# Attention and FFN block: weighted sums in pairs in the halves of one PSUM bank, reciprocals turned in the query fills

## The reference, cut to what matters

```python
q, k, v = layernorm(x) @ wq + bq, ctx @ wk + bk, ctx @ wv + bv   # split into 16 heads
score = (q @ k.T) / sqrt(32) * mask
score = where(score == 0, -1e9, score)
x = x + (softmax(score) @ v) @ wo + bo
w = complex(w_real, w_imag)
x = x + real(ifft(fft(layernorm(x)) @ w)) + bias
```

## Time and profile before

| | |
|---|---|
| median of three runs | 472.79 us |
| the profiled execution | 471.82 us |
| its span in the profile | 470.0 us |
| mean granted TensorE clock | 0.996 of full speed |
| TensorE busy | 449.7 us, 96% |
| VectorE busy | 415.9 us, 88% |
| ScalarE busy | 373.9 us, 80% |
| GpSimd busy | 364.5 us, 78% |

### The profile page before, as it was taken

One profiled execution on the slowest core, in us unless ns is written; L12 is line 12 of the kernel. 1 busy time (PEld: TensorE's weight loads), 2 busy tenths in 40 slices (PEclk: granted clock), 3 DMA queues, 4 the chain that ended last, 5 costly groups with the idle time before them and its releaser, 6 DMA issues.

```text
span 470.0 us, 11312 instructions
## 1 busy us (share of the span) xinstructions
PE 449.7 (96%) x3538; PEld 297.8 (63%) x3538; DVE 415.9 (88%) x698; ACT 373.9 (80%) x1431; POOL 364.5 (78%) x519
## 2 busy tenths in 40 slices
PE   6989879898999999999999999999999999999997
PEld 5777557677566666666666666666666666555543
DVE  3797799999999898989999999989898999999552
ACT  3359559789998889899898988898988898899720
POOL 6589657897989979787979797987979882868562
PEclk9999989999999999999999999999999999999999
DMA  8999902332444554444544545353632432341143
GB/s 284 395 352 294 270 11 67 86 86 68 94 105 117 115 135 114 128 120 119 140 108 113 131 102 158 85 137 103 128 78 71 90 82 74 84 91 44 48 112 113
DMA packets 83308, 59.37 MB, mean 126 GB/s; under 512 B 39729, under 2 KB 70705, under 8 KB 82738
## 3 DMA queue, kind: packets, MB, share of 16 engines
q1 hardware_dynamic: 82816, 58.55, 46.2%
q10 hardware_dynamic: 434, 0.10, 0.1%
HBM read 29.27 MB, written 8.39 MB: 80 GB/s over the span
## 4 chain that ended last, share of the span: by engine, by line
PE 80%; DVE 8%; issue 4%; ACT 3%; DMA 2%; POOL 1%; SPq 0%; DVEq 0%; POOLq 0%
PE bank L396 33%; PE bank L468 16%; PE bank L522 10%; PE bank L539 7%; PE bank L401 5%; PE bank L510 5%; PE bank L535 3%; ACT zs L624 2%; DMA cxs<-in_ctx 2%; DVE zs L784 1%; DVE zs L791 1%; PE bank L471 1%; DVE nmin L796 1%; DVE lp L839 1%; POOL x L1002 1%
## 5 line engine op out<-in xcount | busy, mean ns | idle before, releaser
L624 ACT ACTIVATE zs<-zs,nbias 128x128 f32<-128x128 f32 x512 | 199.8, 397 | 19.7 <-POOL nbias L1016 19.6
L624 ACT ACTIVATION_READ_ACCUMULATOR zs<-zs,nbias 128x1 f32 x512 | 99.6, 194 | 0.0
L791 DVE SCALAR_TENSOR_TENSOR zs<-zs 128x1024 f32<-128x1024 f32 x64 | 91.8, 1435 | 2.3
L784 DVE TENSOR_TENSOR zs<-bank,ms 128x512 f32<-128x512 f32 x128 | 82.0, 682 | 0.0
L796 DVE TENSOR_REDUCE nmin<-zs 128x8 f32<-128x1024 f32 x64 | 77.2, 1206 | 0.1
L633 ACT COPY pt<-bank 128x512 f32<-128x512 f32 x128 | 67.8, 582 | 7.0 <-PE bank L522 6.8
L468 PE MATMUL bank<-xth,wqh 128*128 128x256 f16 x256 | 70.7, 276 | 2.2 <-DVE kl L743 1.8
L468 PE MATMUL bank<-xth,wql 128*128 128x256 f16 x256 | 70.2, 274 | 0.0
L468 PE MATMUL bank<-xtl,wqh 128*128 128x256 f16 x256 | 70.1, 274 | 0.0
L522 PE MATMUL bank<-ident,zs 128*128 128x128 f32 x512 | 66.9, 274 | 1.0 <-ACT zs L624 1.0
L522 PEld LDWEIGHTS bank<-ident,zs 128*128 128x128 f32 x512 | 57.4, 140 | 5.7 <-ACT zs L624 4.4
(11 more groups left out here) (109 smaller groups left out, 954.7 us busy)
## 6 DMA issues: line engine op xcount, KB each, us to landing
xs<-in_x SPq DMA_DIRECT2D x16, 512.0 KB, 4.4
xtr<-in_xt SPq DMA_DIRECT2D x16, 512.0 KB, 5.1
out<-x SPq DMA_DIRECT2D x32, 256.0 KB, 2.5
qs<-qh SPq DMA_DIRECT2D x120, 64.0 KB, 2.0
lp<-in_lparts SPq DMA_DIRECT2D x4, 1024.0 KB, 9.8
qs<-ql SPq DMA_DIRECT2D x60, 64.0 KB, 2.0
ms<-in_mask SPq DMA_DIRECT2D x16, 128.0 KB, 2.4
wqs<-in_wq SPq DMA_DIRECT2D x2, 512.0 KB, 6.4
```

The lines of the kernel that those rows point to most:

```text
L624: last = act.activation(z, z, ACT.Exp, bias=nbias[:, s % 4, i:i + 1], scale=-NEG, accum_out=zsum[:, s % 4, i:i + 1])
L784: dve.tensor_tensor(zs[:, s % NZ, t], A[n % 2][:].rearrange("p (h k) -> p h k", h=4), ms[:, c % NM, t, :].unsqueeze(1).broadcast_to([128, ...
L791: dve.scalar_tensor_tensor(out=z, in0=z, scalar=0.0, in1=z, op0=ALU.is_equal, op1=ALU.subtract).then_inc(eq_done, 1)
```

## The change

- The weighted sums are made two at a time, at the head of even slots: slot v does steps v-4 and v-3, the even step in the lower half of bank CX, the odd one in the upper half. In PE's order they now stand ahead of `turn`. `ctx_norm` of either step waits for both sums, and the next pair waits until both are normed.
- The reciprocals of step v-3 are turned at the end of the last late fill of slot v, into the upper half of that fill's bank. From slot 55 on, where no query is left, a fill `R` holds them alone.
- The upper half of query quarter 2 is no longer free, so the statistics get a fill `ST` of their own just ahead of that quarter.
- ScalarE copies the reciprocals after `copy_pt`, followed by the held fills, and only then does the second half of `exps`. VectorE does `least`, then the held fills, then `ctx_norm`, then `low_m` and the mid fills.

The core of the diff:

```diff
-        late = [("Q",) + f for f in queries.get(v, [divmod(v + 9, 4)]) if f[0] < NC]
+        late = []
+        for f in queries.get(v, [divmod(v + 9, 4)]):
+            if f[1] == 2 and 3 <= f[0] + 1 < NC:
+                late.append(("ST", f[0] + 1))
+            if f[0] < NC:
+                late.append(("Q",) + f)
+        if 0 <= v - 3 < NS and not late:
+            late.append(("R", v - 3))
...
+        if 0 <= v - 3 < NS:
+            turned[v - 3] = len(fills) - 1
         items = []
+        if v % 2 == 0 and 0 <= v - 4 < NS:
+            items += [("PV", v - 4), ("PV", v - 3)]
         if 0 <= v - 2 < NS:
             items += [("PT", v - 2, 0), ("PT", v - 2, 1)]
...
-        if 0 <= v - 3 < NS:
-            items += [("PV", v - 3)]
...
+            def turn_rz(o, s):
+                pe.wait_ge(p_rz, s + 1)
+                for t in range(2):
+                    last = pe.transpose(o[:, 256 + 128 * t:384 + 128 * t], rzb[:, s % 2, 4 * t:4 * t + 4, :], ident[:])
...
+                if n in step_of:
+                    last = turn_rz(o, step_of[n])
...
-                if s >= 1:
-                    pe.wait_ge(cn_done, s)
+                if s >= 2:
+                    pe.wait_ge(cn_done, s - s % 2)
...
-                pe.wait_ge(p_rz, s + 1)
-                for t in range(2):
-                    pe.transpose(CX[:, 256 + 128 * t:384 + 128 * t],
-                                 rzb[:, s % 2, 4 * t:4 * t + 4, :], ident[:])
+                o = slice(256 * (s % 2), 256 * (s % 2) + 256)
...
             def copy_rec(s):
-                act.wait_ge(pv_done, s + 1)
-                act.copy(rec[:, s % 2, :], CX[:, 256:512]).then_inc(rc_done, 1)
+                act.wait_ge(g_done, turned[s] + 1)
+                if s >= 2:
+                    act.wait_ge(cn_done, s - 1)
+                act.copy(rec[:, s % 2, :], G[turned[s] % 3][:, 256:512]).then_inc(rc_done, 1)
...
-                if 0 <= v - 4 < NS:
-                    copy_rec(v - 4)
                 if 2 <= v - 1 < NS:
                     exps(v - 1, 0)
                 if 0 <= v - 2 < NS:
                     copy_pt(v - 2, 0)
                     copy_pt(v - 2, 1)
+                if 0 <= v - 4 < NS:
+                    copy_rec(v - 4)
+                for n in held:
+                    hi(n)
...
-                for n in held + mids:
+                for n in mids:
                     hi(n)
...
                     zero_to_neg(v)
+                if 0 <= v < NS:
+                    least(v)
+                for n in held:
+                    lo(n)
                 if 0 <= v - 4 < NS:
                     ctx_norm(v - 4)
-                if 0 <= v < NS:
-                    least(v)
                 if 0 <= v - 9 < 4:
                     low_m(v - 9)
-                for n in held + mids:
+                for n in mids:
                     lo(n)
...
             def ctx_norm(s):
                 dve.wait_ge(rc_done, s + 1)
+                dve.wait_ge(pv_done, s - s % 2 + 2)
...
             def spread(s):
                 pool.wait_ge(rz_done, s + 1)
                 if s >= 2:
-                    pool.wait_ge(pv_done, s - 1)
+                    pool.wait_ge(g_done, turned[s - 2] + 1)
```

20 lines of the change are left out of this document (10 added, 10 removed).

## The result

The changed kernel takes 489.21 us, the median of three runs (489.07 to 490.04), against 472.79: ratio 1.0345, 95% interval 1.0314 to 1.0377. I had forecast 473.9 and a range that ended at 477.5. The change is 16.4 us slower.

A forecast was written before the change was run, and what follows sets the result against it. TensorE was taken to set the pace in slots 14 to 54, VectorE in slots 4 to 13, VectorE and ScalarE in the last. -3.6 + 5.5 - 0.6 = +1.3 us, rounded to 473.9 us; range 469.0 to 477.5.

The forecast's parts named there:

- the early slots: Slots 4 to 13: new VectorE waits for ScalarE's `od` and `high_m` cost 6.3 us, less 0.8 relief: +5.5.
- the steady slots: Slots 14 to 54, TensorE-paced: pairs save 2.7 us and a vanished product wait 0.9, together -3.6.
- the tail: From slot 55: VectorE's earlier start and two sums in a row at the end save 0.6 us (+0.3 to -1.2).
- The pair: Steady slots on TensorE: two sums in a row save 0.17 us per pair, net 0.14 (bounds -0.02 and 0.17).
- Rival 4: The pair saves nothing because the third batch drains like the first: 476.6 us, chance 0.10.
- DVE's 23.83 of work in what becomes 24.8 us still fits: Steady slots, per four slots: VectorE's work fits the shortened time, so TensorE waits there were taken as 0.
- the far bound of -4.4: Steady slots: the largest saving allowed for pairs and the vanished product wait together, against -3.6 expected.
- rival 3: Statistics slots: the query fill waits for its bank, 0.3 us in each of ten slots: 476.9 us, chance 0.17.
- The pair asks for the product of step v-5 some 1.1 us after it is there: Head of even steady slots: the product is ready before the pair, removing a wait of 0.9 us in all.

The follow-up runs named there:

- d1: d3, with ScalarE also doing `high_m` and the `od` copies ahead of `ctx_hi` in slots 4 to 12: 472.78 us.
- d3: Changed kernel; VectorE's product ahead of `least` and held fills, reciprocals ahead of `copy_pt` from slot 9, `ST` last in its slot (chunk 4: slot 5): 474.5 us.
- b2: Kernel before the change with only the new orders of ScalarE and VectorE, single sums kept: 486.21 us.
- a1: Changed kernel; in slots 4 to 12 ScalarE does `high_m` and the `od` copies ahead of `ctx_hi`: 487.33 us.
- a2: Changed kernel; `ST` placed behind the query quarter in its slot instead of ahead of it: 488.49 us.
- b1: Kernel before the change; only the statistics get their own fill, ahead of query quarter 2: 479.67 us.
- b4: b1, but `ST` stands last in its slot, and that of chunk 4 in slot 5 instead of 6: 473.31 us.
- e2: d1, but from slot 56 on the pair of sums stands behind `turn`: 472.86 us.

## Why the prediction was wrong, point by point

All three terms of the sum failed: the early slots cost 13.5 instead of 5.5, the steady slots lost 1.8 where 3.6 were to be gained, and the tail lost 2.1 where 0.6 was to be gained.

1. **The pair** was right in kind and small in size: 0.25 saved instead of 0.17, 0.19 net instead of 0.14. From the second batch to the third, that is from one sum to the next, it is 0.22, so nothing drains between the two sums. By the rule of the Trainium skill ("TensorEngine Tiling (Array Packing)", Key Properties) a change of the tile alone drains nothing; the trace agrees, with 1.00 for both sums. Rival 4 is out.
2. **The steady gain of 3.6** exists: d1 and d3 gain 4.8 there. The changed kernel doesn't have it, and the step that failed here is one sentence: "DVE's 23.83 of work in what becomes 24.8 us still fits". It took the busy time of before for an order that is not that of before. Two things were missing: 0.45 us per four slots for `least` directly behind the instruction it depends on, and `zero_to_neg` longer by 0.19 in the mean, 0.75 per four slots. What DVE fills of four slots is their length less its waits. Before, that was 25.2 - 1.2 = 24.0, as it waited 12.6 us for `qh` between 135 and 394 us. 24.0 + 0.45 + 0.75 = 25.2 is over the 24.8 that was to be had; the trace after has 25.47 from one group of four slots to the next (265.32 to 290.79), with 0.24 of waits. The single sums of b2, with 25.48, bear it out. How much each of the two things costs by itself no run shows. (A slip beside it: the far bound of -4.4 for the steady slots comes to -4.2 by its own terms, 19.5 x 0.17 and 0.9.) The 0.11 was to be seen in the earlier trace rows: the product there starts and gives way to an instruction that doesn't read it in 0.33, shorter than its own 0.42. I read such distances as the cost of an instruction, where they are also a property of the one behind.
3. **The early waits** (+5.5) were right in place and near in size: 0.74 in slots 4 to 6 and 1.00 to 1.61 in slots 9 to 12 of the trace, with 2.47 in slot 7 and 1.44 in slot 8 beyond it; 5.2 us by a1 and about 6.2 by b2. What failed is the sum around them. The ring of banks in slots 4 to 13 was priced as rival 3, at 0.3 in ten steady slots; in fact the steady slots pay 0.8 for its place (a2), and one early slot pays 3.1 to 3.8 at once (`U` of slot 7 behind `ST`, b1 and b4). I had followed the query of a statistics slot round the ring, but not the mid fill of the slot behind it, which takes the bank of `ST` and is wanted soonest.
4. **The clock** was missing altogether. The earlier trace rows show 0.93 from 57.20 to 82.40 us of the kernel before, and I passed over it. (That stretch is not four slots: `turn` of slot 4 starts at 57.59 and that of slot 8 at 89.24. Over slots 4 to 13 DVE is busy 84.0 of 86.3 us, so the reading of it as nearly full holds.) In the changed kernel 5.2 us more are missing from full clock by slot 16, close behind those holes of PE. That is at most 5.2 of the 13.5, since a part falls where PE is not the bound. With 5.2 for the waits (a1), and 4.2 for the bank (b1, in which some 1.7 are clock), the 13.5 are made up within 1 us, but clock and waits can't be added cleanly.
5. **The tail** (-0.6) had the wrong sign; the table has +2.1. I let the pair come to its slot's head free of charge, though DVE and ACT are full there; PE's sums then wait 6.3 us for the product, in four slots:

```profile
PE bank L555 <- DVE cn L828: 6.3, 4, 1.9
```

"The pair asks for the product of step v-5 some 1.1 us after it is there" holds for the steady stretch only.

The chances put 0.17 on a rival of 476.9, which had the early waits and the bank, but no case also let the steady gain go, though a full DVE doesn't exclude the other two. All three came. With my prices that case would have been 476.9 + 3.6 = 480.5, still 8.7 short of the measured time. So the prices of the early slots were the larger fault, and the list of cases the smaller.

Why the repaired kernels don't beat the kernel before: in the traces the early 3 us take back most of the 4.8, in d1 the tail 1.2 more, and in the runs the clock takes the rest. At a mean granted clock of 0.996 three runs of e2 took 470.26, 471.08 and 471.14, and eight of the kernel before made beside them 471.31 to 472.54. Five of ten of e2 ran at 0.989 (473.46 to 474.94), and only three of twenty of the kernel before at 0.988 (473.38 to 473.95). Why e2 meets the lower clock more often stays open. So does whether the early reciprocals shorten `zero_to_neg` by moving it out of POOL's way: one meeting is shown, its timing was not varied by itself.

## What to carry to other kernels

When work is taken off the engine that bounds, price the second engine in its *new* order, slot by slot, with the price of a dependent neighbour, and hold it against the new, shorter slot. When a ring of buffers gets one more member, walk every fill behind it round the ring once, above all in the slots that are crowded for another reason. And add up the rivals that can all be true at the same time: the slow end of a range is at least their sum, and here even the sum of my prices fell short.

## What the runs showed of the hardware

- A VectorE instruction that reads the result of the one just ahead started 0.034 us behind its recorded end, one that doesn't 0.078 ahead of it (means over some 41 slots of the changed kernel and of the kernel before): 0.11 us for the dependence.
- In the changed kernel `zero_to_neg`, one instruction on operands of one size, took 1.22 to 2.60 us and POOL's `rzb` copy 0.39 to 1.41. In the one meeting shown both were long where they overlapped; `least`, with one input, stayed at 1.22 everywhere.
- A hole on TensorE can be paid twice. Behind 2.41 us of waiting, the stretch from 141 to 145 us of the changed kernel had a granted clock of 0.58, so most of it lay at the 1.2 GHz level, and the sixteen matmuls of a pair took 1.94 us there instead of 1.07. That is some 1.7 us (0.42 x 4) missing from full clock behind a hole of 2.4. It need not come: behind a hole of 2.65 us in b2 (118.4 to 121.1 us) the granted clock stayed at 1.00. The changed kernel:

```profile
140.71 0.28 PE L487 MATMUL bank<-xth,wqh 128*128 128x256 f16 x1 [2.41 <-DVE ql L777]
...
143.19 1.94 PE L555 MATMUL bank<-pt,vs 128*32 128x256 f32 x16
```

- Runs of one kernel differ by the clock: those of e2 took 470.3 to 471.1 at a mean granted clock of 0.996 and 473.5 to 474.9 at 0.989. 0.007 of 470 us is 3.3, about the difference itself.
